# Gated delta rule and ternary feed-forward on one core: the ternary weights' pieces between the first head's, and the convolution by batch

## The reference, cut to what matters

```python
x = L0_attn_x
xn = _layernorm(x)
# attention of layer 0
qkvz = (xn @ W_qkvz).reshape(B, T, HK, 2 * DK + 2 * VR * DV)
ba = (xn @ W_ba).reshape(B, T, HK, 2 * VR)
mixed = concat(q, k, v_pre)                 # along channels
y = silu(conv1d(mixed, conv_w))             # 4 taps, each channel by itself
beta, g = sigmoid(b), -exp(A_log) * softplus(a + dt_bias)
o = chunk_gated_delta_rule(q, k, v, g, beta)   # decay = exp(g_i - g_j), inverse of I + M, a scan over chunks
og = rmsnorm(o * silu(z)) * norm_w
attn = og @ W_out
# feed-forward of layer 0: weights of 2048 x 256 and 256 x 1024
w = w.astype(bfloat16); scale = mean(|w|) over groups of 64
q = clip(round(w / scale), -1, 1); w_hat = w + (q * scale - w)
x = x + attn + ffn(xn, w_hat)
# feed-forward of layer 1: scale = mean(|w|) over the tensor
w_q = sign(w) * (|w| >= 0.7 * scale)
```

## Time and profile before

| | us |
|---|---|
| three runs | 1953.77, 1959.18, 1960.43; median 1959.18 |
| the profiled execution | 1964.37 |
| its span, first to last instruction | 1962.2 |
| first projection of head 0 starts at | 99.56 |
| scaling of head 0's key (L736) / of head 15's | 107.75 / 1401.6, 86.26 a head |
| start of layer 1's first copies of x (L1509) | 1645.79 |
| TensorE / VectorE / ScalarE / GpSimd busy, share of the span | 80% / 53% / 42% / 26% |

### The profile page before, as it was taken

How to read it: one execution, slowest core, us unless ns; L and a number is a source line. 1 busy time by engine, 2 the same in 40 slices (tenths; PEclk the granted TensorE clock), 3 DMA queues, 4 the chain that set the end, 5 groups by cost and what they waited for, 6 DMA issues and landing times. The chain is left out here.

```text
span 1962.2 us, 40518 instructions
## 1 busy us (share of the span) xinstructions
PE 1572.7 (80%) x16552; PEld 1126.9 (57%) x16552; DVE 1034.9 (53%) x1962; ACT 826.6 (42%) x1599; POOL 507.0 (26%) x558
## 2 busy tenths in 40 slices
PE   2165887878878798888888788888969995888999
PEld 2033565656656565665656566665646673454665
DVE  7754646556464655547465554746553314266234
ACT  2143445444445444444544444444434312566300
POOL 5730222312231231313222231222213323310100
PEclk9577899989999998998989898999989997799999
DMA  5221101111010111101111110111030002000200
GB/s 144 79 68 24 36 13 26 47 23 28 10 36 24 26 42 28 26 13 34 26 25 36 35 25 13 33 27 25 12 90 12 1 1 60 1 2 1 65 1 22
DMA packets 187735, 60.89 MB, mean 31 GB/s; under 512 B 153024, under 2 KB 180288, under 8 KB 187296
## 3 DMA queue, kind: packets, MB, share of 16 engines
q1 hardware_dynamic: 169216, 50.30, 11.3%
q10 hardware_dynamic: 18336, 8.01, 1.6%
HBM read 39.21 MB, written 19.07 MB: 30 GB/s over the span
## 5 line engine op out<-in xcount | busy, mean ns | idle before, releaser
L1099 POOL TENSOR_TENSOR og<-og,sz 128x256 f32<-128x256 f32 x128 | 92.9, 726 | 757.3 <-DVE og L1041 532.3
L506 PE MATMUL banks<-wv,xT 128*128 128x512 f32 x256 | 139.9, 698 | 78.6 <-DVE Yv L892 54.1
L892 DVE SCALAR_TENSOR_TENSOR Yv<-banks,cwall,Yv 128x1022 f32<-128x1022 f32 (+2 forms) x96 | 122.3, 1274 | 82.2 <-ACT Yv L736 81.5
L506 PEld LDWEIGHTS banks<-wv,xT 128*128 128x128 f32 x256 | 54.3, 223 | 149.4 <-issue 149.4
L506 PE MATMUL banks<-wqk,xT 128*128 128x512 f32 x256 | 123.7, 628 | 20.2 <-DVE Yk L892 19.6
L869 ACT ACTIVATE V<-banks,skd 128x128 f32<-128x128 f32 x192 | 59.9, 363 | 165.7 <-PE banks L677 165.4
L646 PE MATMUL banks<-wz,xT 128*128 128x256 f32 x512 | 125.5, 389 | 1.4 <-DVE yacc L1061 1.4
L715 PE MATMUL banks<-wo,oT 128*128 128x256 f32 x512 | 122.9, 383 | 0.8 <-ACT oT L885 0.8
L646 PEld LDWEIGHTS banks<-wz,xT 128*128 128x128 f32 x512 | 100.7, 199 | 23.7 <-issue 9.8
L1070 POOL TENSOR_TENSOR E<-E,nsk 128x1024 f32<-128x1024 f32 x32 | 60.9, 1925 | 165.2 <-DVE nsk L919 161.1
L715 PEld LDWEIGHTS banks<-wo,oT 128*128 128x128 f32 x512 | 93.8, 190 | 14.8 <-issue 1.9
(11 more groups left out here) (368 smaller groups left out, 3717.2 us busy)
## 6 DMA issues: line engine op xcount, KB each, us to landing
cm_d<-CM SPq DMA_DIRECT2D x32, 256.0 KB, 3.9
wqk<-in_L_attn_W_qkvz SPq DMA_DIRECT2D x8, 512.0 KB, 4.7
wv<-in_L_attn_W_qkvz SPq DMA_DIRECT2D x8, 512.0 KB, 3.8
wz<-in_L_attn_W_qkvz SPq DMA_DIRECT2D x16, 256.0 KB, 2.8
wo<-in_L_attn_W_out SPq DMA_DIRECT2D x16, 256.0 KB, 3.1
blk<-cm_d SPq DMA_DIRECT2D x128, 16.0 KB, 1.8
t_d<-tb SPq DMA_DIRECT2D x16, 128.0 KB, 1.7
u_d<-ub SPq DMA_DIRECT2D x16, 128.0 KB, 1.8
```

The costliest lines, as they stand in the source:

```text
L506: ins = pe.matmul(bank[b][:, :], xT[:, d, b * S + of_batch, :], w[:, d, :], start=(d == 0), stop=(d == KD - 1))
L892: v.scalar_tensor_tensor(y, pair[0][:, :, 0:T - j], conv_w(k, t)[:, 3 - j:4 - j], y, ALU.mult, ALU.add).then_inc(s["tap"].sem, 1)
L1099: pool.tensor_tensor(og[:, n, :, :], og[:, n, :, :], sz[q % 2][:, b, :].rearrange("p (h d) -> p h d", h=VR), ALU.mult).then_inc(s["osz"].s ...
```

## The change

- **Ternary weights between the first head's pieces.** `GROUPS` and the table `FIRST` are new: group 0 is due at -21, groups 1 to 5 at 5.5 to 48.9, 6 to 9 at 64.5 to 82.5, so they stand between head 0's and head 1's pieces; head 0's `pk` is due at -6, its decays at 6.4 to 7.6 behind the key's projection and ahead of the query's at 11.73. All six casts are issued one after another. `wb` of groups 2 to 5 moves from sz, St and Sd into UB[1], whose fill moves behind group 5's turn (`fill1`). The sums of layer 1's weights (`r1`) are due at -12.32, ahead of the gates' arithmetic (`ba`, -7.96). For groups 6 to 9 VectorE compares once, then compares and subtracts in one instruction; GpSimd's subtraction goes.
- **Convolution weights.** They are loaded as 64 rows of 512 numbers into part of t512; TensorE turns them with four transposes (`cwp`), VectorE copies (`cwe`).
- **Fills.** `fill` is due at -35.37, behind the normalization's -45, on GpSimd's queue directly behind `prs` as before, with one UB fill less.
- **Sigmoid** of beta is issued behind Exp and Ln (`abeta`); the gates' arithmetic waits for the product, and `pgs` for it.
- **Taps by batch.** Projections signal by batch; scaling and taps are one instruction a batch (128x512, 128 x 512 - j), and the next projection's batch waits for its own bank's last tap.
- **Another table of times** `AT` for heads 1 to 14 (`FINAL` stays). Among its moves: on ScalarE `k0` stands ahead of the turned output and the inverse's copies, the query's first square ahead of `V`; on TensorE `KK` stands behind AV of the last lane, `QK` ahead of SU of lane 0, `TU32` ahead of `pk`; on VectorE lane 1's `S` behind `v1`, `UBd` ahead of `S`; SP issues `wv` at 19.22 of its own head where it was due 25 us ahead of it.

```diff
+    cwr = rows.rearrange("p (c j) -> p c j", j=4)
 ...
+        yield START["cwe"]
+        v.wait_ge(*s["cwp"]())
+        v.tensor_copy(m["cwall"][:, :, :], bank[3][:, 0:256].rearrange("p (j h) -> p h j", j=4)).then_inc(s["cwe"].sem, 1)
         yield START["ba"]
         gate = Chain(v, s["pgate"])
-        v.wait_ge(*s["pact"](0))
+        v.wait_ge(*s["pba"]())
 ...
+        yield START["cwp"]
+        pe.wait_ge(*s["pcw"]())
+        pe.wait_ge(*s["const"]())
+        for j in range(4):
+            ins = pe.transpose(bank[3][:, j * 64:(j + 1) * 64], cwr[:, :, j], c["ident"][0:64, 0:64])
+        ins.then_inc(s["cwp"].sem, 1)
 ...
+        pe.wait_ge(*s["pact"](2))
 ...
-        act.dma_start(m["cwall"][:, :, :], a["L0_attn_conv_w"].rearrange("(h p) j -> p h j", p=P)).then_inc(s["psmall"].sem, 16)
+        act.dma_start(cwr[:, :, :], a["L0_attn_conv_w"].rearrange("(h p) j -> h p j", p=P)).then_inc(s["pcw"].sem, 16)
 ...
-        yield START["abeta"]
-        act.wait_ge(*s["pba"]())
-        act.activation(tab[:, :, BETA, :, :], ba[:, :, 0:VR, :], ACT.Sigmoid).then_inc(s["pact"].sem, 1)
 ...
+        yield START["abeta"]
+        act.activation(tab[:, :, BETA, :, :], ba[:, :, 0:VR, :], ACT.Sigmoid).then_inc(s["pact"].sem, 1)
 ...
-GROUPS = (-193.35, -180.0, -167.02, -155.33, -149.06, -121.87, 1.64, 8.58, 11.79, 16.77)
+GROUPS = (-21.28, 5.52, 19.04, 26.77, 39.04, 48.92, 64.48, 68.98, 72.98, 82.46)
 ...
 AT = {
 ...
-    "g": -60.0, "wqk": -55.0, "wv": -25.0, "cm": 22.0, "base": 38.0, "wz": 72.0, "E0": -38.78, "E1": -38.18, "E2": -36.38, "E3": -35.78, "exp0": -38.38, "exp1": -37.78, "exp2": -35.98,
-    "exp3": -35.38, "pk": -13.38, "k0": 6.12, "k1": 7.3, "k2": 8.6, "k3": 9.22, "ks": 11.12, "kT": 13.3, "kt0": 13.91, "kt1": 15.16, "nk": 14.39, "KK": 15.0, "nE0": 16.0, "nE1": 18.24,
+    "g": -58, "wqk": -55.28, "wv": 19.22, "cm": 23.37, "base": 28.86, "wz": 79.25, "E0": -38.44, "E1": -38.18, "E2": -36.73, "E3": -32.43, "exp0": -37.41, "exp1": -36.46, "exp2": -36.44,
+    "exp3": -34.5, "pk": -9.2, "k0": -5.44, "k1": 6.42, "k2": 8.23, "k3": 8.68, "ks": 13.08, "kT": 12.21, "kt0": 13.83, "kt1": 14.89, "nk": 14.74, "KK": 20.71, "nE0": 12.12, "nE1": 16.9,
 ...
 FIRST = {
-    "g": -58.88, "wqk": -199.85, "wv": -177.07, "cm": 22.0, "base": 41.82, "wz": 67.1, "E0": -37.33, "E1": -36.73, "E2": -34.48, "E3": -34.22, "exp0": -40.28, "exp1": -40.26, "exp2": -38.15,
+    "g": 10.7, "wqk": -58.52, "wv": -54, "cm": 23.12, "base": 41.82, "wz": 53.8, "E0": 6.44, "E1": 6.64, "E2": 7.44, "E3": 7.64, "exp0": 6.33, "exp1": 6.53, "exp2": 7.33, "exp3": 7.53,
 ...
-    wb = [line(Yk[1]).bitcast(BF16)[:, i * 1024:(i + 1) * 1024] for i in range(2)] + [line(t).bitcast(BF16) for t in (sz[0], sz[1], St, Sd)]
+    wb = [line(Yk[1]).bitcast(BF16)[:, i * 1024:(i + 1) * 1024] for i in range(2)] + [line(UB[1]).bitcast(BF16)[:, i * 1024:(i + 1) * 1024] for i in range(4)]
 ...
-        if t:
-            pe.wait_ge(*s["tap"](3 * t - 1, k))
-        elif k == 0:
+        if t == 0 and k == 0:
             pe.wait_ge(*s["pxT"]())
-        elif k:
+        elif t == 0:
             pe.wait_ge(*s["vn"](3, k - 1))
         for b in range(B):
+            if t:
+                pe.wait_ge(*s["tap"](6 * t - 2 + b, k))
             for d in range(KD):
                 ins = pe.matmul(bank[b][:, :], xT[:, d, b * S + of_batch, :], w[:, d, :], start=(d == 0), stop=(d == KD - 1))
-        ins.then_inc(s["proj"].sem, 1)
+            ins.then_inc(s["proj"].sem, 1)
 ...
+        for b in range(B):
+            act.wait_ge(*s["proj"](2 * t + b, k))
+            act.activation(Y(t, k)[:, b, :], bank[b][:, :], ACT.Copy, scale=conv_w(k, t)[:, 3:4]).then_inc(s["tap0"].sem, 1)
 ...
-        v.wait_ge(*(s["tap0"](t, k) if j == 1 else s["tap"](3 * t + j - 2, k)))
-        y = Y(t, k)[:, :, j:T]
-        v.scalar_tensor_tensor(y, pair[0][:, :, 0:T - j], conv_w(k, t)[:, 3 - j:4 - j], y, ALU.mult, ALU.add).then_inc(s["tap"].sem, 1)
+        for b in range(B):
+            v.wait_ge(*(s["tap0"](2 * t + b, k) if j == 1 else s["tap"](6 * t + 2 * j - 4 + b, k)))
+            y = Y(t, k)[:, b, j:T]
+            v.scalar_tensor_tensor(y, bank[b][:, 0:T - j], conv_w(k, t)[:, 3 - j:4 - j], y, ALU.mult, ALU.add).then_inc(s["tap"].sem, 1)
 ...
-            yield START["qc"] + GROUPS[g]
+            yield START["qc"] + g
 ...
+            v.wait_ge(*(s["qtp"](g - 2) if g >= 8 else pooled(g - 2)))
+            v.tensor_scalar(low[g % 2], raw[g - 6], s2[:, 2 + i:3 + i], None, ALU.is_le).then_inc(s["qlow"].sem, 1)
             yield START["q1c"] + GROUPS[g] + 0.8
-            v.tensor_scalar(low[g % 2], raw[g - 6], s2[:, 2 + i:3 + i], None, ALU.is_le).then_inc(s["qcmp"].sem, 1)
+            v.wait_ge(*s["qlow"](g - 6))
+            v.scalar_tensor_tensor(tern[g % 2], raw[g - 6], s2[:, i:i + 1], low[g % 2], ALU.is_ge, ALU.subtract).then_inc(s["qcmp"].sem, 1)
 ...
+        pool.memset(UB[0][:, :, :], 0.0).then_inc(s["zero"].sem, 1)
+        yield START["fill1"]
+        pool.wait_ge(*s["qtp"](5))
+        pool.memset(UB[1][:, :, :], 0.0).then_inc(s["zero"].sem, 1)
```

More of the change, by code:

```diff
@@ L151, in constants, with prep @@
     return c
-def prep(s, a, c, bank, m, wide, more, small, ints):
+def prep(s, a, c, bank, m, wide, more, small, ints, rows):
     xa, xT, tab, half = m["yacc"], m["xT"], m["tab"], c["half"]
@@ L429, in gdn @@
     over_group = lambda t, g: t[:, g % 2, :].unsqueeze(2).to_broadcast([P, 16, GR64])
-    start = prep(s, a, c, bank, m, line(E), line(CM), line(Td), line(P4))
+    start = prep(s, a, c, bank, m, line(E), line(CM), line(Td), line(P4), t512[0:(2 + VR) * HK, :])
     at = lambda k: FIRST if k == 0 else FINAL if k == LAST else AT
@@ L547, in pe_turn_v @@
             pe.wait_ge(*s["Y"](3, k))
-            pe.wait_ge(*s["tap"](11, k))
+            pe.wait_ge(*s["tap"](23, k))
         if q >= 2:
@@ L991, in v_inverse @@
             v.wait_ge(*s["TR"](7, k - 2))
+        else:
+            v.wait_ge(*s["zero"](4 + k))
         for g in quarters:
@@ L1205, in pe_turned_weights @@
             src = wb[g] if g < 6 else tern[g % 2]
-            pe.wait_ge(*pooled(g))
+            pe.wait_ge(*(pooled(g) if g < 6 else s["qcmp"](g)))
             if g >= 2:
@@ L1352, in pool_fill @@
         pool.memset(Tf[:, :, :], 0.0).then_inc(s["zero"].sem, 1)
-        for i in range(2):
-            pool.memset(UB[i][:, :, :], 0.0).then_inc(s["zero"].sem, 1)
+        pool.memset(UB[0][:, :, :], 0.0).then_inc(s["zero"].sem, 1)
+        yield START["fill1"]
+        pool.wait_ge(*s["qtp"](5))
+        pool.memset(UB[1][:, :, :], 0.0).then_inc(s["zero"].sem, 1)
     def on_gpsimd(pool):
```

71 lines of the change are left out of this document (31 added, 40 removed), and 37 rows, old and new, of tables (AT, FIRST, START, s).

## The result

Four runs of the changed kernel: 1904.15, 1904.75, 1910.49 and 1916.19 us, median **1907.6** (forecast 1905); four to eleven runs of the kernel before beside each set have medians of 1956.5 to 1962.2. The ratio is 0.976, 95% interval 0.973 to 0.979: faster. The profiled execution took 1910.5 (forecast 1910), its span is 1908.8.

A forecast was written before the change was run, and what follows sets the result against it. TensorE's in-order queue was taken to bound the loop over heads, something else the first 100 us. Start 33 plus loop 21 gave 54 us off 1964.4: 1910 profiled, median 1905, range 1880 to 1938.

The forecast's parts named there:

- Start: Launch to head 1's query projection: ternary groups no longer all precede head 0; 33 us gained, bounds 15 and 41.
- contention in the substitution: Head 0's substitution on VectorE slowed beside GpSimd's work on group 3: 6.2 us lost, between 0 and 8.5.
- The stall on ScalarE's queue: At launch, ScalarE's third small transfer held 20.18 us behind the convolution weights; the changed load removes it.
- Contention as a rival (2): Head 0: VectorE and GpSimd exclude each other over groups 3 to 5, pieces on the chain; total 1923 or 1938; chance 0.14.
- Loop: The 14 further heads: taps by batch and new order shorten TensorE's waits; 21 us, bounds nothing and 50 us.
- I take 1.5 us a head: The gain adopted for each of 14 further heads, 21 us together; at most 3.6 a head.
- 0.9, 0.9 net and 1.5: Waits saved per head, in us, before the query, third and fourth projections on TensorE.
- Rival 1: Heads' waits return at GpSimd and the recurrence, so the 14 further heads give nothing; 1926 us; chance 0.22.
- More than forecast (3): Fourth projection's shorter wait keeps the clock high, 1.2 us a head, and the substitution meets no contention; 1876 us; chance 0.15.
- The end: The last layer, which the change leaves alone; no gain or loss counted.
- Rival 5: Launch: GpSimd's fills still run beside the normalization, already in the sum; truly behind it, 5 us more; no chance given.
- Slower (4): New order on TensorE and ScalarE costs 4.5 us in each of 14 heads; 1989 us; chance 0.05.

The follow-up runs named there:

- Half taps: Heads 2 to 14 get the earlier kernel's table of times, taps by batch and start stay, against the changed kernel; 1917.2 us, ratio 0.974-0.983.
- whole taps: Scaling and taps one instruction for both batches again, new table and start kept, against the changed kernel; 1926.1 us, ratio 0.977-0.986.
- the one new order tried: Silu of z and products A moved earlier in heads 1 to 14, head 15's first part reordered, against the changed kernel; 1912.2 us, ratio 0.973-0.979.

## Why the prediction was right, and where it wasn't

- **Start: right, and by its steps.** 33 us forecast, 33.2 measured; no named time of the chain was off by more than 4 us. Two errors inside cancel: contention in the substitution cost 8.2 us (forecast 6.2, bound 8.5), and the steps ahead of it came 2 to 4 us sooner. The stall on ScalarE's queue, which looked the largest item, is worth 4 us alone. What brought head 0's query projection forward by 50 us is that the six groups no longer stand ahead of it; the rows show this, no run takes it by itself.
- **Contention as a rival (2): the mechanism is there**, on the chain as it said (6.7 us for group 3, 5.8 for the fills), but small beside the 33. One of its rows was misread: the 0.42 us at 50.28 in the earlier trace rows stand while GpSimd is idle. The comparison holds by another row of the kernel before, with a PSUM input and GpSimd busy (36.15 to 39.34):

```profile
37.40 0.42 DVE L231 TENSOR_TENSOR CM<-banks,Td 128x256 f32<-128x256 f32 x1
```

- **Loop: the releaser right, size and balance wrong.** The step that failed is "I take 1.5 us a head": heads 2 to 14 gave 2.8, the fourteen together 29.9 us instead of 21, their last being 2.9 us longer than before. The prediction's own items (0.9, 0.9 net and 1.5) add up to 3.3 us, and it gives no reason for taking less than half. That TensorE's waits did shrink by 3.3 is luck again: 6.4 us a head went (5.1 of the taps, all 2.8 ahead of the fourth projection where 1.5 was forecast, and og's 1.3, which was to grow), and 3.1 came back at z's silu, V and A, where 0.6 was forecast, at og. TensorE's busy time then took 0.5 us a head of it in this profile; between nine profiles of the same loop it runs from 0.6 less than before to 0.6 more. Half taps or order alone would have given 1.3 or 1.0. Rival 1 was wrong as a whole, though about half of what went did return.
- **More than forecast (3)**: its condition came true, its gain didn't. All fourth projections are at the higher clock, but the lower one moved ahead of them (0.82 instead of 0.89 from third to fourth), and of the 1.2 us a head that the clock was to give back TensorE's busy time shows nothing (73.5 us; 73.0 before). The nine profiles of this loop have 0.82 to 0.86 there.
- **The end: taken as nothing, it cost 9.7 us** of the profiled execution. Of this 8.3 is layer 1 at a lower clock. Of the thirteen profiles with most or all of the change five have layer 1 at 316.4 to 317.4, as before, eight at 319.0 to 325.5. So the change doesn't force it. The loop's surplus hid it: that the total came within 2.6 us of the forecast it owes to these two, by luck.
- **Rival 5 was right in all parts**: the fills do run beside the normalization, and moving them gives 5.8 us.
- **Slower (4)**: the heads didn't get longer, but for the first and last of the fourteen periods (0.6 and 2.9 us). That the order costs busy time, 0.7 us a head with whole taps, is hinted at by one profile and not shown.

What decides which executions have layer 1 at the lower clock stays open, and whether the denser loop makes it more likely: each kernel has one profile here, and the kernel before only one. Why the lower clock moved ahead of the fourth projection stays open too.

## What to carry to other kernels

When a wait on the bounding engine goes, list the other chains that end within the same stretch before you count it: here each removed wait uncovered the next, and the last to be found, a round trip through memory, did not yield to the one new order tried. Take the engine's busy time over the same heads together with its waits: one short projection, or one slow one, doesn't tell what the clock did. Put GpSimd's long elementwise work where VectorE has nothing on the chain, or only operations that read PSUM (0.42 us beside GpSimd above); a due time in a queue doesn't ensure that, a wait does. And cut both traces at common events before you call a total understood: this one was right to 3 us with two parts wrong by 9 and 10 us.
